# A fused network kernel's convolution prepared in two halves of 16 heads

## The reference

```python
# L0 cond: a convolution over 512 positions; 32 heads, 64 modes each, 64 rows of length 512
dt = exp(log_dt); A = -exp(log_A_real) + 1j * A_imag; dtA = A * dt[:, None]
P = dtA[:, :, None] * arange(512)
Cs = Cc * (exp(dtA) - 1) / A
K = 2 * einsum('hn,hnl->hl', Cs, exp(P)).real      # the taps, 32 x 512
y = irfft(rfft(K, 1024) * rfft(u * mask, 1024))[..., :512] + u * mask * D
y = y * mask
# L0 ffn: x = x + y @ (fp8 weight * scale).T
# L1 cond: each of 64 blocks of tokens times the weight of its adapter (one of 16)
# L1 ffn: w1, w2, w3 (1376 hidden) are quantised to NF4 in blocks of 64 and back, then
x = x + (silu(x_ @ w1.T) * (x_ @ w2.T)) @ w3.T
```

## Time and profile before

| | us |
|---|---|
| median of 3 runs | 952.16 |
| lowest, highest | 951.54, 956.98 |
| the profiled execution | 951.24 |
| its span | 949.5 |

### The profile page before, as it was taken

One profiled execution on the slowest core, in us unless ns is written; L12 is line 12 of the kernel. 1 busy time (PEld: TensorE's weight loads), 2 busy tenths in 40 slices (PEclk: granted clock), 3 DMA queues, 4 the chain that ended last, 5 costly groups with the idle time before them and its releaser, 6 DMA issues.

```text
span 949.5 us, 10316 instructions
## 1 busy us (share of the span) xinstructions
PE 885.1 (93%) x3261; PEld 474.5 (50%) x3262; DVE 579.8 (61%) x880; ACT 390.1 (41%) x458; POOL 86.9 (9%) x127
## 2 busy tenths in 40 slices
PE   0299998999999999999999999999989999899998
PEld 0296448998444444444444444444434555354442
DVE  7889977886998888888997300000132354158444
ACT  2024637876777776676687100000012132241200
POOL 5100009600000000000000000002201011100000
PEclk9999998999999999999999999999999999999999
DMA  6873127562000000000000300024010000002022
GB/s 203 317 242 134 74 81 246 195 223 70 23 22 23 17 31 0 31 30 1 30 1 0 87 13 1 0 72 136 1 45 1 1 1 1 1 1 44 0 89 88
DMA packets 32967, 61.19 MB, mean 64 GB/s; under 512 B 5880, under 2 KB 8264, under 8 KB 31704
## 3 DMA queue, kind: packets, MB, share of 16 engines
q1 hardware_dynamic: 32216, 60.50, 18.8%
q0 software_dynamic: 704, 0.10, 0.3%
HBM read 51.07 MB, written 8.47 MB: 63 GB/s over the span
## 4 chain that ended last, share of the span: by engine, by line
PE 83%; DVE 12%; issue 2%; DMA 1%; ACT 1%; POOLq 1%; POOL 0%; SPq 0%; ACTq 0%; DVEq 0%
PE ps L820 81%; DVE acc L1374 2%; DVE T L1374 2%; PE ps L861 1%; DVE W2T L1218 1%; PE ps L1075 1%; DVE W2T L1224 1%; POOLq L603 1%; DVE W2T L1221 1%; DVE raw L1352 0%; DVE amax L1345 0%; DMA T<-kpad 0%; DVE W1T L1218 0%; DVE Up L1551 0%; DVE Yp L1659 0%
## 5 line engine op out<-in xcount | busy, mean ns | idle before, releaser
L652 ACT ACTIVATE above<-raw,cst 128x1024 bf16<-128x1024 f32 (+2 forms) x225 | 271.8, 1231 | 122.1 <-DVE acc L1374 46.5
L820 PE MATMUL ps<-Yp,W3T 128*128 (+2 forms) x872 | 183.9, 367 | 6.6 <-POOL Yp L605 2.6
L1374 DVE SCALAR_TENSOR_TENSOR acc<-above,acc 128x1024 f32<-128x1024 bf16 (+2 forms) x112 | 148.1, 1323 | 18.3 <-ACT above L652 11.6
L820 PE MATMUL ps<-Up,W1T 128*128 128x512 f32 x344 | 155.5, 594 | 3.0 <-DVE Up L1473 1.9
L820 PE MATMUL ps<-Up,W2T 128*128 128x512 f32 (+1 forms) x392 | 155.1, 593 | 0.0
L820 PEld LDWEIGHTS ps<-Yp,W3T 128*128 128x128 f32 (+1 forms) x872 | 121.9, 196 | 63.7 <-issue 61.5
L1374 DVE SCALAR_TENSOR_TENSOR T<-above,T 128x1024 f32<-128x1024 bf16 (+1 forms) x84 | 114.1, 1359 | 20.9 <-ACT above L652 18.0
L820 PE MATMUL ps<-X,W3T 128*128 128x512 f32 (+1 forms) x256 | 113.7, 602 | 0.6 <-DVE Yp L1659 0.6
L820 PEld LDWEIGHTS ps<-Up,W2T 128*128 128x128 f32 (+1 forms) x392 | 64.2, 177 | 83.0 <-issue 83.0
L820 PEld LDWEIGHTS ps<-Up,W1T 128*128 128x128 f32 x344 | 64.1, 190 | 82.5 <-issue 76.3
L1495 DVE TENSOR_TENSOR X<-X,Yp x16 | 4.6, 349 | 125.6 <-issue 125.6
(11 more groups left out here) (299 smaller groups left out, 753.4 us busy)
## 6 DMA issues: line engine op xcount, KB each, us to landing
W3T<-in_wa SPq DMA_DIRECT2D x11, 1024.0 KB, 6.3
raw<-in_w SPq DMA_DIRECT2D x20, 256.0 KB, 3.3
W3T<-kpad SPq DMA_DIRECT2D x9, 512.0 KB, 5.0
Up<-in_xconv SPq DMA_DIRECT2D x4, 1024.0 KB, 11.5
X<-in_xT SPq DMA_DIRECT2D x1, 4096.0 KB, 22.9
xkeep<-X SPq DMA_DIRECT2D x4, 1024.0 KB, 4.5
X<-xkeep SPq DMA_DIRECT2D x4, 1024.0 KB, 9.6
W3T<-in_wa SPq DMA_DIRECT2D x5, 768.0 KB, 4.6
```

The source lines that it names most:

```text
L652: nc.scalar.activation(above[0:h, m % 2, 0:w], raw[0:h, u % 2, 0:w], ACT.Relu, scale=STEEP, bias=cst[0:h, C_BND + i:C_BND + i + 1]).then_i ...
L820: return nc.tensor.matmul(o, l, r, start=start, stop=stop, **kw)
L1374: V.scalar_tensor_tensor(out=ac, in0=src, scalar=float(STEPS[i]), in1=ac, op0=ALU.min, op1=ALU.add).then_inc(s["m_used"], 1)
```

## The change

The taps are made in two halves f of 16 heads, f = 0 for heads 0 to 15. VectorE's angles, whole turns, factors and skip term, ScalarE's last sine, TensorE's small products and SyncE's stores are each done per half. The second half uses PSUM bank 7. VectorE's order becomes: angles and turns of half 0, coefficients, factors 0, angles 1, skip term 0, turns 1, the ids' ranks, factors 1, start of unit 0, skip term 1, the adapter order. TensorE's small products of half 1 stand in front of the wait for u and the first strip. SyncE stores half 0, loads strips 0 to 4, stores half 1, loads the others; each strip from group 8 on waits for its store of half 1.

The decoding of w0 moves from before the adapter order to behind the convolution output of group 3, unit 1's load from strip 4 to strip 14. X, one load of 4 MB before the stores, becomes four of 1 MB: two at the old place, one behind strip 8, one behind strip 12. NCV, NF0, NAD go from 10, 26, 50 to 4, 28, 54. The skip vector's four small loads follow the heads' new places.

```diff
-        NCV, NF0, NAD = 10, 26, 50
+        NCV, NF0, NAD = 4, 28, 54
...
             load_unit(0)
-            sp.dma_start(X[:, :, :], A["xT"].rearrange("(c p) n -> p c n", p=P)).then_inc(s["l_x"], 16)
+            load_x(0)
+            load_x(1)
...
-            sp.wait_ge(s["d_k"], 1)
-            for q in range(4):
-                sp.dma_start(kr[:, q * HQ:(q + 1) * HQ, :], ksb[q * 32:q * 32 + LA, :, :]).then_inc(s[f"l_kp{q}"], 16)
+            def store_k(f):
+                sp.wait_ge(s["d_k"], f + 1)
+                for q in range(4):
+                    h = f * HF + q * HE
+                    sp.dma_start(kr[:, h:h + HE, :], ksb[q * 32:q * 32 + LA, f * HE:(f + 1) * HE, :]).then_inc(s[f"l_k{'pq'[f]}{q}"], 16)
+
+            store_k(0)
             sp.wait_ge(s["l_kpz"], 16)
             for g in range(HG):
...
-                if g * GH % HQ == 0:
-                    sp.wait_ge(s[f"l_kp{g * GH // HQ}"], 16)
+                if g * GH % HE == 0:
+                    sp.wait_ge(s[f"l_k{'pq'[g * GH // HF]}{g * GH // HE % 4}"], 16)
...
                 if g == NS - 1:
+                    store_k(1)
+                if g == HG - 2:
                     sp.wait_ge(s["d_w0"], 1)
                     load_unit(1)
 
+                if g in (8, 12):
+                    load_x((8, 12).index(g) + 2)
...
-            act.wait_ge(s["d_ang"], 2)
-            nc.scalar.activation(trig, whole, ACT.Sin, scale=-turn1).then_inc(s["a_ang"], 1)
+            for f in range(2):
+                hs = slice(f * HF, (f + 1) * HF)
+                act.wait_ge(s["d_ang"], f + 2)
+                nc.scalar.activation(trig[:, hs, :], whole[:, hs, :], ACT.Sin, scale=-turn1).then_inc(s["a_ang"], 1)
...
+            pe.wait_ge(s["d_kz"], 2)
+            def make_k(f):
+
+                pe.wait_ge(s["d_pp"], f + 1)
+                for i in range(HE):
+                    for q in range(4):
+                        h = f * HF + q * HE + i
+                        last = mm(ps[q * 32:q * 32 + LA, 6 + f, i * LC:(i + 1) * LC], pc[:, h, :], trig[:, h, 0:LC], True, True)
+                last.then_inc(s["p_k"], 1)
+
+            make_k(0)
...
+            make_k(1)
             pe.wait_ge(s["l_u"], 16 * DC)
             for g in range(HG):
...
+            angles(0)
+            whole_turns(0)
             expm1(a_, sl_[18], True, [sl_[19], sl_[20], sl_[21], sl_[22]])
...
+            def factors(f):
+
+                hs = slice(f * HF, (f + 1) * HF)
+                dve.wait_ge(s["a_ang"], 5 + f)
+                tt(trig[:, hs, 0:LC], trig[:, hs, 0:LC], dec[:, hs, 0:LC], ALU.mult)
+                tt(pc[:, hs, :], trig[:, hs, CMULT:], al[:, hs].unsqueeze(2).to_broadcast([P, HF, LA]), ALU.mult)
+                tt(pq[:, hs, :], trig[:, hs, LC:CMULT], be[:, hs].unsqueeze(2).to_broadcast([P, HF, LA]), ALU.mult)
+                tt(pc[:, hs, :], pc[:, hs, :], pq[:, hs, :], ALU.add)
+                V.tensor_tensor(pc[:, hs, :], pc[:, hs, :], dec[:, hs, LC:], ALU.mult).then_inc(s["d_pp"], 1)
...
+            factors(0)
+            angles(1)
+            skip_term(0)
+            whole_turns(1)
 
             dve.wait_ge(s["l_ids"], 32)
...
+            factors(1)
...
             start_unit(0)
-            dve.wait_ge(s["l_w0"], 32)
...
+            skip_term(1)
             dve.wait_ge(s["p_ord"], 1)
...
                 for k in parts_of(K_CONV, g):
                     level(k)
                 conv_out(g)
-            dve.wait_ge(s["l_x"], 16)
+                if g == 3:
+                    dequantise_w0()
+                    dve.wait_ge(s["d_w0"], 1)
+            dve.wait_ge(s["l_x"], 16 * DC)
```

More of the change, by code:

```diff
@@ L143, in build @@
         n0 += 2 * S * LA
-        HQ = S // 4
+        HQ, HF, HE = S // 4, S // 2, S // 8
         ksb = w2f[:, n0:n0 + HQ * LC].rearrange("p (h m) -> p h m", h=HQ)
@@ L305, in build @@
         s = {}
-        for n in """l_zq g_xs a_xs d_nrm m_ready m_used g_nrm d_xs p_w16 a_rk a_v2 p_rke a_kk g_pad d_wz p_va a_va p_lgt a_lgt l_l3 a_w16 d_w16 d_ak d_rmx a_fo g_x2 l_cst l_s4 l_s5 l_w0 l_u l_x l_len l_ids l_kpz l_kp0 l_kp1 l_kp2 l_kp3 l_dsk g_dsk d_kz l_keep l_back l_strip0 l_strip1 l_strip2 l_strip3 l_strip4 l_raw0 l_raw1 l_wa0 l_wa1 l_wa2 l_late l_prep l_l3w
+        for n in """l_zq g_xs a_xs d_nrm m_ready m_used g_nrm d_xs p_w16 a_rk a_v2 p_rke a_kk g_pad d_wz p_va a_va p_lgt a_lgt l_l3 a_w16 d_w16 d_ak d_rmx a_fo g_x2 l_cst l_s4 l_s5 l_w0 l_u l_x l_len l_ids l_kpz l_kp0 l_kp1 l_kp2 l_kp3 l_kq0 l_kq1 l_kq2 l_kq3 l_dsk g_dsk d_kz l_keep l_back l_strip0 l_strip1 l_strip2 l_strip3 l_strip4 l_raw0 l_raw1 l_wa0 l_wa1 l_wa2 l_late l_prep l_l3w
                 l_sml l_diag l_bm l_out d_sl
@@ L463, in load_unit, with load_x @@
                                      ).then_inc(got, 16)
+            def load_x(c):
+                sp.dma_start(X[:, c, :], A["xT"][c * P:(c + 1) * P, :]).then_inc(s["l_x"], 16)
             load_unit(0)
-            sp.dma_start(X[:, :, :], A["xT"].rearrange("(c p) n -> p c n", p=P)).then_inc(s["l_x"], 16)
+            load_x(0)
+            load_x(1)
             kv = kpad.ap()
@@ L856, in turn_unit @@
                     elif n + m < 2:
-                        pe.wait_ge(s["d_k"], 1)
+                        pe.wait_ge(s["d_k"], 2)
                     else:
@@ L1227, in _ @@
             V.memset(zpad, 0.0).then_inc(s["d_zp0"], 1)
-            V.memset(ps[:, 6, 0:HQ * LC], 0.0).then_inc(s["d_kz"], 1)
+            for f in range(2):
+                V.memset(ps[:, 6 + f, 0:HE * LC], 0.0).then_inc(s["d_kz"], 1)
             dve.wait_ge(s["l_s4"], 80)
@@ L1271, in _, with angles, whole_turns @@
             V.tensor_tensor(dec, a_.unsqueeze(2).to_broadcast([P, S, CMULT]), mul, ALU.mult).then_inc(s["d_ang"], 1)
[L1272 to L1277, removed]
+            def angles(f):
+                hs = slice(f * HF, (f + 1) * HF)
+                tt(trig[:, hs, 0:CMULT], f_[:, hs].unsqueeze(2).to_broadcast([P, HF, CMULT]), mul[:, hs, :], ALU.mult)
+            def whole_turns(f):
+                hs = slice(f * HF, (f + 1) * HF)
+                ts(trig[:, hs, CMULT:], trig[:, hs, LC:CMULT], 0.25, None, ALU.add, ALU.bypass)
+                ts(trig[0:MODES, hs, 0:LC], trig[0:MODES, hs, 0:LC], 0.25, None, ALU.add, ALU.bypass)
+                ts(whole[:, hs, :], trig[:, hs, :], ROUND, None, ALU.add, ALU.bypass)
+                V.scalar_tensor_tensor(out=whole[:, hs, :], in0=whole[:, hs, :], scalar=ROUND, in1=trig[:, hs, :],
+                                       op0=ALU.subtract, op1=ALU.subtract).then_inc(s["d_ang"], 1)
+            angles(0)
+            whole_turns(0)
             expm1(a_, sl_[18], True, [sl_[19], sl_[20], sl_[21], sl_[22]])
@@ L1311, in _, with skip_term @@
             ts(be[hi], cr[hi], -2.0, None, ALU.mult, ALU.bypass)
[L1312 to L1321, removed]
+            def factors(f):
+                hs = slice(f * HF, (f + 1) * HF)
+                dve.wait_ge(s["a_ang"], 5 + f)
[4 more added lines that the diff above has]
+                V.tensor_tensor(pc[:, hs, :], pc[:, hs, :], dec[:, hs, LC:], ALU.mult).then_inc(s["d_pp"], 1)
+            def skip_term(f):
+                o = slice(f * HE, (f + 1) * HE)
+                dve.wait_ge(s["p_k"], f + 1)
+                dve.wait_ge(s["g_dsk"], 3)
+                V.tensor_tensor(ksb[:, o, :], ps[:, 6 + f, 0:HE * LC].rearrange("p (h c) -> p h c", c=LC), kdk[:, o, :], ALU.add
+                                ).then_inc(s["d_k"], 1)
+            factors(0)
+            angles(1)
+            skip_term(0)
+            whole_turns(1)
             dve.wait_ge(s["l_ids"], 32)
@@ L1363, in level @@
                         dve.wait_ge(s[f"l_kp{q}"], 16)
+                        dve.wait_ge(s[f"l_kq{q}"], 16)
                 if i == 0 and banks_before(u):
@@ L1428, in _, with dequantise_w0 @@
                 link(V.tensor_scalar(mnat[:, c, :], lenf[:, 0, :], cst[:, C_L + c:C_L + c + 1], None, ALU.is_gt))
+            def dequantise_w0():
+                dve.wait_ge(s["l_w0"], 32)
+                link(V.tensor_copy(h16a, w0u))
+                link(V.tensor_scalar(h16b, h16a, 0x7F, 7, ALU.bitwise_and, ALU.logical_shift_left))
+                link(V.tensor_scalar(h16a, h16a, 0x80, 8, ALU.bitwise_and, ALU.logical_shift_left))
+                link(V.tensor_tensor(h16a, h16a, h16b, ALU.bitwise_or))
+                V.tensor_scalar(w0, h16a.bitcast(f16), 256.0, None, ALU.mult).then_inc(s["d_w0"], 1)
             for g in range(HG):
```

4 lines of the change are left out of this document (2 added, 2 removed).

## The result

| | before | changed |
|---|---|---|
| median of 20 runs each, us | 953.68 | 957.96 |
| lowest, highest | 950.24, 957.51 | 953.40, 960.32 |
| profiled execution, its span | 951.24, 949.5 | 960.19, 958.4 |
| granted clock, mean over the profiled span | 0.992 | 0.982 |

The ratio is 1.0038, 95% interval 1.0022 to 1.0054: by it the kernel is 3.6 us slower (4.3 by the medians), where 3.6 us faster was forecast. The median lies 4 us above the range for 8 in 10 (945.3 to 954), and 8 above the own range's 950. By the 1% bound it is "the same", which had 0.91.

What follows compares the result with a forecast made beforehand. TensorE, busy 93% of the span, was taken as the bound, idle mainly before the first strip product at 42.24. FFN0 3.9 us earlier minus 0.3 in the adapter stage gives 3.6 off; forecast 948.0 us, own range 945.5 to 950.

Steps and rivals of the forecast that it cites:

- Preparation, transfers: Before the convolution: halves and X's split load start the first strip product at 38.8 instead of 42.24, 3.4 us earlier.
- Convolution: Convolution stage: TensorE needs 40.56 us, 0.5 more is gained at its end, FFN0 starts at 80.5, 3.9 us earlier.
- w0's decoding: In the convolution: VectorE's 6.7 us end at 58.4, covered by 5 us before TensorE's eleventh group at 65.
- FFN0: Stage after the convolution: stays TensorE's at 57.0 us with 28 levels; margin 0.7 at the turn of unit 1.
- Adapter stage: Four more levels and a fourth unit start cost 0.3 us; the end bears about 4 us of lateness for nothing.
- the 8.2: Adapter stage: 8.2 us of added VectorE work, four levels of 1.27 and a unit start of 3.2.
- The wait for unit 3's data: Adapter stage: VectorE waits 2 to 4 us because unit 3's load is issued behind adapter weights and X's last store.
- Rival A: Adapter stage: ScalarE's queue holds levels behind outputs TensorE hasn't finished, the 8.2 us come on top, 955.5; chance 0.13.
- theory C: Whole kernel, posed after the result: the time follows TensorE's granted clock, not the schedule; no chance given.
- B: Convolution: X's last 2.1 MB or the extra stores starve the strips, TensorE waits 5.0 us, 952.3; chance 0.07.
- D: Preparation: the second half isn't last, strips at 37.6 decide the start, 946.1; chance 0.06.
- its C: Preparation: padding or taps still land at 37.5, strips at 42, gain 0.5 us or less, 951; chance 0.06.

Runs made afterwards that it cites:

- xfront: Changed kernel with all four loads of X at the front, ahead of padding and taps; 963.4 us, ratio 1.0112 to the kernel before.
- early3: Changed kernel with unit 3's load issued behind the third store of X in FFN0; 950.5 us, ratio 0.9972 to the kernel before.
- levels_early: Kernel before with levels 4, 28, 54 and unit 3's load behind the third store of X in FFN0; 955.0 us, ratio 1.0014.
- hole: Kernel before with one more TensorE wait ahead of up(0), on VectorE's level 82; 962.9 us, ratio 1.0082.
- levels: Kernel before with only the numbers of levels changed from 10, 26, 50 to 4, 28, 54; 958.7 us, ratio 1.0056.
- mix: Changed kernel with levels 8, 28, 50 and unit 1's load at strip 10 instead of 14; 947.5 us, ratio 0.9924 to the kernel before.
- halves: Changed kernel with levels 10, 26, 50, w0 decoded ahead of the adapter order, unit 1 loaded at strip 4; 952.7 us, ratio 0.9994.

## Why the prediction was wrong

**Preparation, transfers: right.** First strip product 38.4 (38.8), released by the second small products; X's halved load in front was worth what was said: with X whole there, xfront's first product starts 4.4 us later.

**Convolution: right.** FFN0 at 80.98 (80.5). The start was 0.4 us earlier than forecast, and the convolution 0.9 longer, 41.5 us against 40.56: its first two groups took 7.78 us against 6.87, all later ones the same. At such a start single matmuls take twice as long as later (3.89 us for 11 in the row at 38.40, against 7.38 for 48 at 46.02), though the profile gives a granted clock of 1.00; how long that lasts differs between executions (6.20 to 7.94 us for the two groups). w0's decoding stayed covered.

**FFN0: right.** 57.0 us, and no hole at the turn of unit 1, for which I had 0.7 us of margin.

**Adapter stage: wrong, and this is the step that failed.** I wrote of ScalarE's 15.0 us of waits for TensorE that "these waits take up the 8.2", and that TensorE "stalls only when an output is over 3 x 3.57 = 10.7 us late", because it has four PSUM slots. Inside the stage that came nearly true: one stall on an output, 1.31 us at 224.80. But of the 15.0 us 0.6 were left, and at the stage's end up(0) waits for all outputs (L918 of the kernel before), the last included. The forecast let the end bear "about 4 us of this for nothing"; the row of the kernel before has 2.98 us ahead of the last output, and the lateness that arrived there went beyond it by 3.44. The wait for unit 3's data was forecast at 2 to 4 us and measured at 4.44. In all the term put at 0.3 us measured 4.9: 3.1 of it by the late load (early3), the rest by the work that was put there (levels_early keeps a hole of 1.84), with one dip of uncertainty between the two. Rival A, which had 0.13, has the sign, the hole and the late unit 3, but not the mechanism: it held the levels back behind outputs that TensorE hadn't finished, and here the outputs come late behind the levels. Its price of 8.2 was too high for the stage.

The Trainium skill's fit (DMA: Bandwidth & Descriptors, Anatomy of one DMA), which the prediction set beside its row, is given there for transfers on the gpsimd path. SyncE issued these: what it put at 8.0 us took 10.7 (138.43 to 149.1).

**The clock: missing from the sum.** I counted a hole by its length. Here a hole of 3.4 us in front of up(0) takes 2.8 us more in the first product. The schedule up to up(0) gives -3.4 + 4.9 = 1.5 us; the ratio says 3.6, and the profiled execution, which has those four dips, 8.9. The run named hole shows with nothing else changed that a hole can cost more than itself: 3.5 us of hole, 7.8 us of time.

The clock after the result, theory C, therefore doesn't fall altogether. Eleven of the changed kernel's twenty runs have a mean clock of 0.981 or 0.982; of the 75 runs of the kernel before that were taken beside the experiments none is under 0.984. Where the clocks meet, at 0.986 to 0.988, five runs of the changed kernel took 954.57 to 956.12 us, and twelve of the kernel before, beside early3, 953.95 to 957.56: no loss is to be seen there. What falls is C as the only cause: at 0.988 early3's four runs took 950.37 to 952.58 and the changed kernel's three 954.57 to 956.12, and levels and levels_early differ by the place of one load alone. These groups were formed after the fact, and a hole itself lowers the clock, so they bound the schedule's part and don't measure it.

By the Trainium skill (TensorE: Matmul & The Clock Gate, What's actually happening) an idle TensorE is set back to 1.2 GHz, and the gate doesn't begin anew with a kernel, so that the same program meets it at another point in each execution. The rows agree in part. Ahead of up(0) 1.13 us idle brought no dip, 3.44 and 3.49 did, and the runs of one kernel fall on a few values of the clock. But 3.25 us idle ahead of mix's first adapter product, at 140.87, brought none, and 1.9 us ahead of the product at 480 us brought one in one kernel and none in another. Why dips come at 680 us, where TensorE isn't idle in any of these profiles, no run here shows.

The prediction's rivals B and D didn't happen; its C (a late start) is what xfront makes.

What stays open: how much of the late dips is due to the shift of the whole program against the gate, and how much to the hole. In single profiles neither goes with the other: levels has the hole but not the dips at 480 and 680, halves has such dips and no hole. The lower mean clock over the six runs of hole is the only sign that the two are tied.

## What to carry to other kernels

When one says that buffers absorb lateness, ask where they are drained: the first instruction behind the loop that waits for all of them has only the last output's slack (2.98 us here), and lateness that the loop carries along arrives there. When numbers in a hand-written schedule move, look at what else is placed by the same numbers (here a load that slid from a quiet stage into the busiest queue), and move work to an engine's measured idle time, not to the next stage. Price an idle stretch of TensorE with the dip that may follow it: here 3.5 us of it cost 7.8 (5.0 to 10.7), and 1.1 us cost nothing that could be measured. And before a difference of 0.5% is put down to a schedule, compare the mean granted clocks of the runs.

## What was not expected of the hardware

A hole of 3.49 us costs 7.8 us by the ratio, one of 1.13 us 0.3 (within the noise). Dips of the granted clock of about 1.7 us each sit at points where TensorE is busy throughout, such as 676 to 684 us of the changed kernel's profile, and they come in some kernels' profiles and not in others', where the program at that place is the same.

The adapter stage, with the same levels and products, took 89.3 us before, 87.3 in halves and 86.3 in mix; the clock there was 0.96, 0.98 and 1.00. And the first two groups of the convolution took between 6.20 and 7.94 us, at half the later rate for part of it, with a granted clock of 1.00 in the profile.
